# Batch norm and the next layer's products as one stage, with features along the partitions

## The chip, the cores and the metric

The kernel runs on one core of a Trainium2 chip. The metric is the time on the device in microseconds (us), the median of several runs. A core has five engines, each with its own instruction stream: TensorE (PE, with PEld for its weight loads), VectorE (DVE), ScalarE (ACT), GpSimd (POOL) and SyncE (SP). They meet only through semaphores. SyncE and GpSimd issue the DMAs here.

## The reference, cut to what matters

The program runs four graph networks one after the other over 3125 nodes of 256 features and 50000 edges. The change is in the last of them, which has three layers:

```python
for l in range(thetas.shape[0]):
    xi = x[src]
    xj = x[dst]
    e = jax.nn.relu((xj - xi) @ thetas[l].T + xi @ phis[l].T)
    agg = jax.ops.segment_max(e, src, num_segments=N)
    agg = jnp.where(agg < -1e+30, 0.0, agg)
    mu = agg.mean(axis=0)
    var = agg.var(axis=0)
    x = jax.nn.relu((agg - mu) * jax.lax.rsqrt(var + BN_EPS) * gammas[l] + betas[l])
```

Behind it come a residual sum and a layer norm: `x = _layernorm(x + ...)`. The mean and the variance go over the nodes, one of each per feature.

## The kernel before

The nodes lie in 25 tiles of 128 (the last one has 53), each tile with its nodes along the partitions and 256 features behind one another: `X`, `AGG`, `C` and `Y` hold 25 such tiles. Since `xj @ theta` depends on one node alone, a layer forms two products per node. `AGG = x @ theta` goes to a table in memory (`T`), from which the edges gather rows, and `C = x @ (phi - theta)`, the node's own term, stays and is added after the maximum.

Each layer has three stages, and all engines leave a stage together:

- `node_products` (n6, n7, n8 for the three layers). VectorE makes the input rows of a tile, TensorE turns them (two transposes of 128 columns), ScalarE copies them out of PSUM, TensorE makes both products (four matmuls with 256 columns, of which fp32 makes eight records), ScalarE and VectorE copy one product each. For n7 and n8 the rows are made by `stage_normed`, which multiplies by the factor, adds beta and takes the positive part, three VectorE instructions a tile (L1535, L1537, L1539). Every five tiles SyncE stores a piece of the table (L1212).
- `edge_pass` (e5, e6, e7). GpSimd issues 392 indirect gathers of 128 rows each (L1288) into 24 buffers; VectorE runs a maximum over them (L1337); SyncE stores four at a time (L1271). TensorE and ScalarE have nothing to do in these three passes.
- `batch_norm` (bn0, bn1, bn2). GpSimd gathers the maximum of each node (L1447), one DMA a tile. Sums that cross from one partition's chain to the next are mended: VectorE makes a selection matrix (L1497), TensorE multiplies it with the carried rows (L1471), VectorE takes the maximum (L1007). Every five tiles VectorE adds `C` and takes the positive part (L1513, L1514), and TensorE sums over the nodes by a product with ones (L1456). Then the mean is taken off in five wide instructions (L1519), ScalarE squares (L1485), TensorE sums again (L1456), and the factor is made of 256 columns (L1522 to L1526).

Behind bn2 the stage `layer_norm` (ln3) applies the factor and the shift, adds to `X` and takes the row statistics, five tiles at a time (L1417 to L1381), then finds all factors, scales all 25 tiles on ScalarE (L1398), and then stores the output by two DMAs (L1406, L1407).

Of the kernel before, what the change touches and what calls it, by code (L numbers as in the profile page):

```python
# [4 lines left out]
F32 = mybir.dt.float32  # L5
# [8 lines left out]
P = 128  # L14
# [136 lines left out]
def build(nc, a, out):  # L151
    top = ExitStack()
    Stage.used = []
    with top:
# [79 lines left out]
        GAM, BET = sb("GAM", [P, LAYERS, D]), sb("BET", [P, LAYERS, D])  # L234
# [42 lines left out]
        def setup():  # L277
# [17 lines left out]
            with Stage(nc, "set") as st:  # L295
# [43 lines left out]
                def _(eng):  # L339
# [23 lines left out]
                    def spread_row(dst, src, width):  # L363
# [6 lines left out]
                    spread_row(GAM[:, :, :].rearrange("p l d -> p (l d)"),  # L370
                               a["L3_gnn_gammas"].rearrange("(o l) d -> o (l d)", o=1), LAYERS * D)
                    spread_row(BET[:, :, :].rearrange("p l d -> p (l d)"),
                               a["L3_gnn_betas"].rearrange("(o l) d -> o (l d)", o=1), LAYERS * D)
# [973 lines left out]
        def layer_norm(name, prepare, gather=None, out_rows=None):  # L1347

            u = NODE_UNROLL
            with Stage(nc, name) as st:  # L1350
                names = ("chain", "aggregated", "rooted", "scaled", "done", "stored", "apart")
                chain, aggregated, rooted, scaled, done, stored, apart = (st.sem(n) for n in names)
                got = gathered[0:NT // u]
                block = st.block()

                if gather is not None:
                    @block.gpsimd
                    def _(eng):
                        rows, index = gather
                        for t in range(NT):  # L1360
                            got[t % u].arrived(eng, t // u)
                            eng.indirect_dma_start(AGG[:, t, :], None, rows,
                                                   bass.IndirectOffsetOnAxis(ap=index[:, t:t + 1], axis=0)).then_inc(got[t % u].sem, 16)

                @block.vector
                def _(eng):
                    c = Count(eng, chain)
                    with c.loop(NT // u, LINKS[prepare] + 3) as i:
                        if gather is not None:
                            for k in range(u):  # L1370
                                got[k].arrived(eng, i + 1)
                        prepare(c, ds(i * u, u))
                        eng.sem_inc(apart, 1)
                        for j in range(u):
                            last = eng.bn_stats(BS[:, j, :], X[:, ds(i * u + j, 1), :].rearrange("p o d -> p (o d)"))  # L1375
                        c.link(last)
                        eng.sem_inc(apart, 1)
                        for j in range(u):
                            last = eng.bn_aggr(MV5[:, j, :], BS[:, j, :])  # L1379
                        c.link(last)  # L1380
                        c.link(eng.tensor_copy(MV[:, ds(i * u, u), :], MV5[:, :, :]))  # L1381
                    c.link(eng.tensor_scalar(RST[:, :], MV[:, :, 1], EPS, None, ALU.add))
                    eng.sem_inc(aggregated, 1)
                    eng.wait_ge(rooted, 1)
                    c.link(eng.reciprocal(RST[:, :], RST[:, :]))  # L1385
                    c.link(eng.tensor_tensor(NMR[:, :], MV[:, :, 0], RST[:, :], ALU.mult))
                    c.link(eng.tensor_scalar(NMR[:, :], NMR[:, :], -1.0, None, ALU.mult))
                    eng.sem_inc(scaled, 1)

                @block.scalar  # L1390
                def _(eng):
                    eng.wait_ge(aggregated, 1)
                    eng.activation(RST[:, :], RST[:, :], ACT.Sqrt).then_inc(rooted, 1)
                    eng.wait_ge(scaled, 1)
                    with eng.Fori(0, NT // u) as i:  # L1395
                        for j in range(u):
                            t = i * u + j
                            last = eng.activation(tile_of(X, t), tile_of(X, t), ACT.Identity,  # L1398
                                                  bias=NMR[:, ds(t, 1)], scale=RST[:, ds(t, 1)])
                        last.then_inc(done, 1)  # L1400

                if out_rows is not None:
                    @block.sync
                    def _(eng):
                        eng.wait_ge(done, NT // u)
                        eng.dma_start(out_rows[0:(NT - 1) * P, :].rearrange("(t p) d -> p t d", p=P), X[:, 0:NT - 1, :]).then_inc(stored, 16)  # L1406
                        eng.dma_start(out_rows[(NT - 1) * P:N, :], X[0:LAST, NT - 1, :]).then_inc(stored, 16)  # L1407
                        eng.wait_ge(stored, 32)
            if gather is not None:
                for g in got:  # L1410
                    g.close(NODE_UNROLL)


        def last(c, at):

# [10 lines left out]
        def batch_norm(name, layer, gather):  # L1426
# [3 lines left out]
            with Stage(nc, name) as st:  # L1430
# [19 lines left out]
                def column_sums(eng, dst, src, ready, in_front=lambda t: None):  # L1450
                    for t in range(NT):
                        in_front(t + u)
                        if t % u == 0:
                            eng.wait_ge(ready, t // u + 1)
# [481 lines left out]
```

## Time and profile before

| | us |
|---|---|
| median of 3 runs | 5130.29 (5123.8 to 5138.38) |
| the profiled execution, its own time | 5124.81 |
| its span | 5123.1 |
| TensorE busy | 1578.3 (31%) |
| VectorE busy | 3141.9 (61%) |
| ScalarE busy | 1014.3 (20%) |
| GpSimd busy | 3322.2 (65%) |

The busy times are sums over stages that have different limits, so a change in one stage is read from that stage's part of the timeline. A row of the timeline gives the start, the duration of a group, the engine, the line, what is written and read, how many instructions, and in brackets how long the engine was idle before it and what released it. The duration of a pipelined instruction reaches over the start of the next one, so paces are read from starts.

### The profile page before, as it was taken

Reading aid. Unit: us, or ns where it says so; the run is one execution under the profiler, and the core shown is the slowest. Engines: PE = TensorE matmul, PEld = TensorE weight load, DVE = VectorE, ACT = ScalarE, POOL = GpSimd, SP = SyncE. Lnnn points to the kernel's source line nnn. Section 1 sums busy time; section 2 is a strip of 40 time slices with the busy share of each in tenths; the row PEclk is TensorE's granted clock in tenths of the full one; section 3 lists DMA queues with packets and bytes.
Section 4 is the critical chain, followed back from the end, with each engine's and each line's share of the span. In section 5 each row is a group of like instructions: output and inputs, shape, how many; then the busy total and the mean of one; then the engine's idle time right before and its main releaser. Section 6 shows DMA issues by size and latency. Waiting matters only on the chain. (4 is left out here: it accounts for less than half of the span.)

```text
span 5123.1 us, 34834 instructions
## 1 busy us (share of the span) xinstructions
PE 1578.3 (31%) x6898; PEld 1040.1 (20%) x6898; DVE 3141.9 (61%) x9163; ACT 1014.3 (20%) x2570; POOL 3322.2 (65%) x3435
## 2 busy tenths in 40 slices
PE   5220175557555575555400014000070000700002
PEld 5110053335333352222300013000050000500002
DVE  5897566556556579998688887333353333533335
ACT  3333334443444440000311122000010000100001
POOL 3777757774777737777577760777727777177771
PEclk8555575557555595555755557555585555855556
DMA  2766546664666516665366650666516665166661
GB/s 94 229 198 222 189 145 207 208 209 130 202 207 209 193 54 205 205 205 190 91 218 221 222 176 31 201 205 207 192 51 201 207 204 192 49 201 205 205 194 48
DMA packets 318311, 898.86 MB, mean 175 GB/s; under 512 B 73771, under 2 KB 109976, under 8 KB 317976
## 3 DMA queue, kind: packets, MB, share of 16 engines
q0 software_dynamic: 161760, 439.40, 30.8%
q1 hardware_dynamic: 156344, 457.31, 23.9%
q14 instruction: 152, 1.25, 0.1%
q8 instruction: 55, 0.90, 0.1%
HBM read 450.64 MB, written 445.80 MB: 175 GB/s over the span
## 5 line engine op out<-in xcount | busy, mean ns | idle before, releaser
L1288 POOL DMA_INDIRECT WORK<-table,SRCI x1568 | 1512.3, 964 | 638.4 <-issue 512.3
L1288 POOL DMA_INDIRECT WORK<-table,BYSRC x1176 | 1145.6, 974 | 673.0 <-issue 451.0
L1337 DVE SCALAR_TENSOR_TENSOR WORK<-WORK,LOWE 128x256 f32<-128x256 f32 x1564 | 762.9, 488 | 964.4 <-DMA WORK<-table,BYSRC 892.4
L1337 DVE SCALAR_TENSOR_TENSOR WORK<-WORK,NST,e_mv 128x256 f32<-128x256 f32 x1173 | 563.2, 480 | 499.7 <-ACT e_mv L1307 260.2
L1307 ACT ACTIVATE e_mv<-WORK,WE 128x256 f32<-128x256 f32 x1176 | 491.3, 463 | 833.6 <-DMA WORK<-table,SRCI 795.3
L991 PE MATMUL bn_e<-ident,WORK 128*128 128x128 f32 x6 | 2.0, 434 | 1546.2 <-PEq L148 1546.2
L1626 POOL DMA_INDIRECT WORK<-table_attention,SRCI x392 | 373.3, 952 | 119.4 <-issue 119.4
L991 PEld LDWEIGHTS bn_e<-ident,WORK 128*128 128x128 f32 x6 | 0.9, 204 | 1547.3 <-issue 1547.3
L1481 ACT ACTIVATE WORK<-bn_e 128x256 f32<-128x256 f32 x3 | 1.2, 384 | 1551.2 <-PE bn_e L1002 1551.2
L962 PE MATMUL e_hi<-ARENA 128*128 128x392 bf16 x392 | 205.5, 524 | 229.1 <-DVE ARENA L948 229.1
L898 PE MATMUL e_rb<-ARENA 98*128 98x128 bf16 x392 | 114.7, 293 | 444.6 <-ACT ARENA L914 444.6
L900 PE MATMUL e_ra<-ARENA 98*128 98x32 f32 x784 | 249.0, 412 | 0.0
L962 PE MATMUL e_lo<-ARENA 128*128 128x392 bf16 x392 | 208.0, 531 | 0.0
L900 PEld LDWEIGHTS e_ra<-ARENA 98*128 98x128 f32 x784 | 196.2, 310 | 45.8
L898 PEld LDWEIGHTS e_rb<-ARENA 98*128 98x128 bf16 x392 | 95.8, 244 | 462.6 <-ACT ARENA L914 462.6
L1751 DVE SCALAR_TENSOR_TENSOR WORK<-WORK,NST,att_g 128x256 f32<-128x256 f32 x343 | 165.0, 481 | 21.2 <-DVE att_g L1734 10.4
L1158 PE MATMUL n_m<-TURNED,WORK 128*128 128x256 f32 x600 | 163.1, 397 | 0.0
L1786 PE MATMUL comb<-ident,WORK 128*8 128x128 f32 x1 | 0.4, 369 | 527.6 <-PEq L148 527.6
L1162 PE MATMUL n_m<-TURNED,WORK 128*128 128x256 f32 x600 | 155.6, 382 | 0.0
L888 PE MATMUL e_rt<-identb,ARENA 128*98 128x128 bf16 x392 | 132.5, 338 | 12.3 <-DVE ARENA L263 12.3
L1145 PE MATMUL n_x<-WORK 128*128 128x256 f32 x200 | 72.5, 453 | 206.6 <-DVE WORK L1062 198.3
L947 DVE TENSOR_SCALAR ARENA<-iota_b,ARENA 128x128 bf16<-128x128 bf16 x392 | 129.3, 330 | 0.0
(351 smaller groups left out, 4308.5 us busy)
## 6 DMA issues: line engine op xcount, KB each, us to landing
edge_results<-WORK SPq DMA_DIRECT2D x686, 512.0 KB, 3.2
edge_results_attention<-WORK SPq DMA_DIRECT2D x98, 544.0 KB, 3.2
WORK<-table,SRCI POOLq DMA_INDIRECT x1568, 2.9
table<-ARENA SPq DMA_DIRECT2D x35, 640.0 KB, 3.2
WORK<-table,BYSRC POOLq DMA_INDIRECT x1176, 2.9
WORK<-table_attention,SRCI POOLq DMA_INDIRECT x392, 3.3
table_attention<-ARENA SPq DMA_DIRECT2D x5, 660.0 KB
out<-X SPq DMA_DIRECT2D x1, 3072.0 KB
```

The costliest lines, as they stand in the source:

```text
L888: eng.transpose(turned_hot[0:HI, 0, n * P:(n + 1) * P], rank_hi[:, b, n, :], identb[:, :])
L898: eng.matmul(pb[:, cols], rank_t[0:HI, b, 0, cols], rank_t[0:HI, b, 0, cols], start=True, stop=False)
L900: last = eng.matmul(pa[:, n * LO:(n + 1) * LO], rank_tf[0:HI, b, cols], HIST[0:HI, ds((k + first) * RB + n, 1), :].rearrange("p o l -> p ( ...
L947: eng.tensor_scalar(oh_pay[:, b, n, 0, :], iota_b[:, :], place_lo[:, ds(t, 1)], pay_hi[:, ds(t, 1)], ALU.is_equal, ALU.mult)
L962: last = eng.matmul(sums[d][:, :], oh_pay[:, q % 2, n, d, :], oh_place[:, q % 2, n, :], start=False, stop=False)
L1158: last = eng.matmul(mps[:, t % 4, 0:D], XT[:, slot, k * P:(k + 1) * P], w1[:, k, :], start=k == 0, stop=k == 1)
L1162: last = eng.matmul(mps[:, t % 4, D:D + n2], XT[:, slot, k * P:(k + 1) * P], w2[:, k, :], start=k == 0, stop=k == 1)
L1288: eng.indirect_dma_start(G[:, q * GT + k, 0:D], None, T, bass.IndirectOffsetOnAxis(ap=index[:, t:t + 1], axis=0)).then_inc(got[q].sem, 16)
L1307: last = eng.activation(bank[:, k * D:(k + 1) * D], G[:, first + k, 0:D], ACT.Copy, scale=WE[:, ds(g * GT + (2 * h + k), 1)])
L1337: eng.scalar_tensor_tensor(O[:, q % OB, k, :], behind, mask[:, ds(g * GT + k, 1)], here, op0, op1).then_inc(linked, 1)
L1626: eng.indirect_dma_start(G[:, q * GT + k, :], None, T2, bass.IndirectOffsetOnAxis(ap=SRCI[:, t:t + 1], axis=0)).then_inc(got[q].sem, 16)
L1751: eng.scalar_tensor_tensor(OA[:, i, t, 0:D], OA[:, i, t - 1, 0:D] if t else scaled_row, NST[:, ds(b * BT + t, 1)], here, ALU.mult, ALU.add ...
```

## The change

In the third network's place in the order nothing moves up to n6 and e5. Then:

- bn0 and n7 become one stage, and so do bn1 and n8. bn2 and ln3 become one stage too.
- In the first part of the new stage TensorE turns each tile as soon as it is mended: a product of a block of `AGG` with the identity, and on top of it the same for `C`, so that the addition of `C` is made in PSUM. ScalarE takes the positive part on the way out, into `YT`, which has features along the partitions. VectorE takes the sums by `bn_stats` over 512 nodes at a time.
- Then factor and shift are two numbers per partition. ScalarE applies both and the positive part in ten instructions, and `YT` is already turned as the next product wants it.
- Only the product for the table is made in the stage. The own term's product and its copy to `C` are made beside the next edge pass, on TensorE and ScalarE (`own_term_beside`).
- In the last layer TensorE turns the tiles back, VectorE adds them to `X`, and the layer norm goes by fives with a store behind each five.
- gammas and betas are loaded as single numbers down the partitions instead of as rows spread over all partitions.

```diff
-                    spread_row(GAM[:, :, :].rearrange("p l d -> p (l d)"),
-                               a["L3_gnn_gammas"].rearrange("(o l) d -> o (l d)", o=1), LAYERS * D)
...
+                        eng.dma_start(GAMT[:, :], a["L3_gnn_gammas"].rearrange("l (k p) -> p (l k)", p=P)).then_inc(rest_in, 16)
+                        eng.dma_start(BETT[:, :], a["L3_gnn_betas"].rearrange("l (k p) -> p (l k)", p=P)).then_inc(rest_in, 16)
...
+                    def turn(t):
+                        n = P if t < NT - 1 else LAST
+                        eng.wait_ge(mended, t + 1)
+                        if t >= 2:
+                            eng.wait_ge(evicted, t - 1)
+                        for k in range(2):
+                            at = slice(k * P, (k + 1) * P)
+                            eng.matmul(tps[:, t % 2, at], AGG[0:n, t, at], ident[0:n, :], start=True, stop=False)
+                            last = eng.matmul(tps[:, t % 2, at], C[0:n, t, at], ident[0:n, :], start=False, stop=True)
+                        last.then_inc(turned, 1)
...
                     for t in range(NT):
...
+                        nodes = slice(t * P, (t + 1) * P)
                         if t % u == 0:
...
+                            eng.wait_ge(normed, (t // u + 1) * 2)
+                        if t >= 4:
+                            eng.wait_ge(moved, t - 3)
+                        for k in range(2):
+                            if w1 is not None:
+                                last = eng.matmul(ps[:, t % 4, 0:D], YT[:, k, nodes], w1[:, k, :], start=k == 0, stop=k == 1)
+                            else:
+                                last = eng.transpose(ps[:, t % 4, k * P:(k + 1) * P], YT[:, k, nodes], ident[:, :])
...
+                    eng.wait_ge(rooted, 3)
+                    for c in range(NT // u):
+                        nodes = slice(c * u * P, (c + 1) * u * P)
+                        for k in range(2):
+                            eng.activation(YT[:, k, nodes], YT[:, k, nodes], ACT.Relu, bias=BF[:, k, 1:2], scale=BF[:, k, 0:1]).then_inc(normed, 1)
+                    if w1 is None:
+                        for c in range(NT // u):
+                            at = slice(c * u, (c + 1) * u)
+                            eng.wait_ge(spread, c + 1)
+                            eng.activation(RST[:, at], RST[:, at], ACT.Sqrt).then_inc(rooted_rows, 1)
+                            eng.wait_ge(scaled_rows, c + 1)
+                            for t in range(c * u, (c + 1) * u):
+                                eng.activation(X[:, t, :], X[:, t, :], ACT.Identity, bias=NMR[:, t:t + 1], scale=RST[:, t:t + 1]).then_inc(done, 1)
...
+                    def sums(j):
+
+                        eng.wait_ge(evicted, min(4 * j + 4, NT))
+                        for k in range(2):
+                            c.inc(eng.bn_stats(BNS[:, k, j, :], YT[:, k, 4 * j * P:min((4 * j + 4) * P, N)]))
...
+                    def rows_of(k):
+                        for t in range(k * u, (k + 1) * u):
+                            eng.wait_ge(made, t + 1)
+                            eng.tensor_tensor(X[:, t, :], ps[:, t % 4, 0:D], X[:, t, :], ALU.add).then_inc(moved, 1)
+                        eng.wait_ge(moved, (k + 1) * u)
+                        for j in range(u):
+                            last = c.inc(eng.bn_stats(BS[:, j, :], X[:, k * u + j, :]))
+                        c.wait()
+                        for j in range(u):
+                            c.inc(eng.bn_aggr(MV[:, k * u + j, :], BS[:, j, :]))
...
                     for k in range(NT // u):
...
+                        rows_of(k)
+                        if k:
+                            factors_of(k - 1)
+                    factors_of(NT // u - 1)
...
+                def on_tensor(eng):
+                    def multiply(g, q, turn):
+                        if g < NT:
+                            if g >= 2:
+                                eng.wait_ge(moved, g - 1)
+                            for k in range(2):
+                                last = eng.matmul(own[:, g % 2, 0:D], YT[:, k, g * P:(g + 1) * P], DF3[:, layer, k, :], start=k == 0, stop=k == 1)
+                            last.then_inc(made, 1)
```

On TensorE, at the start of bn0, the order before alternates a selection's product (L1471, of 256 columns) with a column sum (L1456):

```order
L991 MATMUL bn_e<-ident,WORK 128x128 x2
L1002 MATMUL bn_e<-ident,WORK 128x128 x2
L1471 MATMUL bn_x<-WORK 128x256 x6
L1456 MATMUL bn_ps<-ARENA,ones 128x256
L1471 MATMUL bn_x<-WORK 128x256
L1456 MATMUL bn_ps<-ARENA,ones 128x256
L1471 MATMUL bn_x<-WORK 128x256
```

On TensorE at the same place the order after has, for each selection's product (L1384), four products of 128 columns with the identity (`bn_t` is the turned tile, L1393 from `AGG`, L1394 from `C`):

```order
L990 MATMUL bn_ps<-ident,WORK 128x128 x2
L1001 MATMUL bn_ps<-ident,WORK 128x128 x2
L1384 MATMUL bn_ps<-WORK 128x256 x2
L1393 MATMUL bn_t<-ident,ARENA 128x128
L1394 MATMUL bn_t<-ident,ARENA 128x128
L1393 MATMUL bn_t<-ident,ARENA 128x128
L1394 MATMUL bn_t<-ident,ARENA 128x128
L1384 MATMUL bn_ps<-WORK 128x256
L1393 MATMUL bn_t<-ident,ARENA 128x128
```

So the column sums have gone and four short products stand in each tile's place. On ScalarE the whole of the new stage and the piece beside the edge pass stand in a few rows, where n7 alone had two copies a tile before (L1418 copies the carried rows, L1421 takes the tile out of PSUM, L1424 is the root, L1429 applies factor and shift, L1551 is the own term's copy):

```order
L1418 ACTIVATE WORK<-bn_ps 128x256
L1421 ACTIVATE ARENA<-bn_t 128x2x128 x25
L1424 ACTIVATE BF<-BF 128x2
L1429 ACTIVATE ARENA<-ARENA,BF 128x640 x10
L148 UNCONDITIONAL_BRANCH
L1298 UNCONDITIONAL_BRANCH
L1551 ACTIVATE ARENA<-e_own 128x256 x25
```

The copies of the table's product are no longer among them: VectorE makes them now (L1483). On TensorE, at the start of n7, the order before was this, for each tile two transposes and both products (L1158 the table's, L1162 the own term's):

```order
L1151 MATMUL n_t<-ident,WORK 128x128 x4
L1158 MATMUL n_m<-TURNED,WORK 128x256 x2
L1162 MATMUL n_m<-TURNED,WORK 128x256 x2
L1151 MATMUL n_t<-ident,WORK 128x128 x2
L1158 MATMUL n_m<-TURNED,WORK 128x256 x2
L1162 MATMUL n_m<-TURNED,WORK 128x256 x2
```

and after, the 25 products for the table (two matmuls each) stand behind the last turned tile, and the own term's 50 matmuls have moved into the next edge pass:

```order
L1393 MATMUL bn_t<-ident,ARENA 128x128
L1394 MATMUL bn_t<-ident,ARENA 128x128
L1410 MATMUL bn_ps<-TURNED,ARENA 128x256 x50
L148 UNCONDITIONAL_BRANCH
L1290 UNCONDITIONAL_BRANCH
L1543 MATMUL e_own<-TURNED,ARENA 128x256 x50
```

The transposes of n7 are gone, and the own term's products stand in a stage in which TensorE had no row before.

## Rows read from the trace of the kernel before

**Rows 1.** Windows: start:end, length, PE, PEld, DVE, ACT, POOL busy (count), clock, DMA, GB/s
```profile
3706.80:3753.00 46.20, 29.37 (x104) 21.72 (x104) 29.29 (x63) 0.38 (x1) 26.33 (x25) 0.81 0.24 71
3753.00:3774.00 21.00, 14.13 (x50) 11.39 (x50) 9.88 (x9) 6.77 (x6) 0.00 (x0) 0.79 0.00 1
3774.00:3836.60 62.60, 53.09 (x250) 41.52 (x250) 36.97 (x100) 17.86 (x50) 0.02 (x1) 0.94 0.15 53
4989.30:5055.00 65.70, 42.48 (x154) 32.36 (x154) 39.01 (x71) 7.15 (x7) 25.60 (x25) 0.83 0.17 51
5055.00:5096.00 41.00, 0.00 (x0) 0.00 (x0) 34.68 (x73) 0.22 (x1) 0.00 (x0) 0.51 0.00 0
5109.00:5123.00 14.00, 0.00 (x0) 0.00 (x0) 0.00 (x0) 0.14 (x1) 0.00 (x0) 0.50 0.69 229
```

**Rows 2.** Timeline of GpSimd and VectorE as the first batch norm begins
```profile
3707.56 0.94 POOL L1447 DMA_INDIRECT ARENA<-edge_results,end_src  x1 [9.53 <-SPq L148]
...
3712.55 0.94 POOL L1447 DMA_INDIRECT ARENA<-edge_results,end_src  x1 [0.30 <-issue]
...
3715.48 0.48 DVE L1007 SCALAR_TENSOR_TENSOR ARENA<-bn_x,ALONE,ARENA 128x256 f32<-128x256 f32 x1 [6.22 <-DMA ARENA<-edge_results,end_src]
...
3716.07 0.48 DVE L1007 SCALAR_TENSOR_TENSOR ARENA<-bn_x,ALONE,ARENA 128x256 f32<-128x256 f32 x1
```

**Rows 3.** Timeline of TensorE: products of 256 columns, then selections beside loads
```profile
3056.17 0.69 PE L1794 MATMUL comb_x<-WORK 128*128 128x264 f32 x2
...
3056.69 0.29 PE L1795 MATMUL comb_x<-WORK 128*128 128x8 f32 x2
...
3056.83 0.69 PE L1794 MATMUL comb_x<-WORK 128*128 128x264 f32 x2
...
3829.24 1.03 PE L1158 MATMUL n_m<-TURNED,WORK 128*128 128x256 f32 x4
...
3830.10 1.03 PE L1162 MATMUL n_m<-TURNED,WORK 128*128 128x256 f32 x4
```

**Rows 4.** Windows of the batch norm's first part, columns as in rows 1
```profile
3721.00:3725.00 4.00, 4.00 (x11) 3.29 (x12) 1.60 (x5) 0.00 (x0) 3.03 (x4) 0.58 0.33 98
3725.00:3740.00 15.00, 10.40 (x48) 8.51 (x47) 12.46 (x28) 0.00 (x0) 11.90 (x11) 1.00 0.33 97
```

**Rows 5.** Timeline of TensorE: the 25 column sums of squares after a pause
```profile
3756.07 14.13 PE L1456 MATMUL bn_ps<-ARENA,ones 128*128 128x256 f32 x50 [3.34 <-ACT ARENA L1485]
```

**Rows 6.** Timeline of ScalarE and VectorE: squares, a row's statistics, the factors, the scaling
```profile
3754.74 6.88 ACT L1485 ACTIVATE ARENA<-ARENA 128x1280 f32<-128x1280 f32 x5 [45.28 <-DVE ARENA L1519]
...
5060.51 1.73 DVE L1375 BATCH_NORM_STATS2 BS<-X 128x6 f32 x5
5062.38 0.45 DVE L1379 BATCH_NORM_AGGREGATE MV<-BS 128x2 f32<-128x6 f32 x5
...
5095.07 0.18 DVE L1382 TENSOR_SCALAR ROWSUMS<-ROWSUMS 128x25 f32<-128x25 f32 x1 [0.21 <-DVE ROWSUMS L1381]
...
5096.76 12.39 ACT L1398 ACTIVATE X<-X,ROWSUMS  x25 [1.19 <-DVEq L1388]
```

**Rows 7.** Timeline: the last copy of a product, and the next pass's first gather
```profile
3831.69 0.42 DVE L1900 COPY ARENA<-n_m 128x256 f32<-128x256 f32 x1 [1.30 <-ACT ARENA L1545]
3836.58 0.94 POOL L1288 DMA_INDIRECT WORK<-table,BYSRC  x1 [95.39 <-PEq L148]
```

**Rows 8.** Timeline of GpSimd: first and last gather of passes one and six
```profile
120.74 1.12 POOL L1288 DMA_INDIRECT WORK<-table,SRCI  x1 [36.80 <-issue]
...
613.99 0.94 POOL L1288 DMA_INDIRECT WORK<-table,SRCI  x1 [0.30 <-issue]
...
4336.01 1.12 POOL L1288 DMA_INDIRECT WORK<-table,BYSRC  x1 [0.30 <-issue]
```

**Rows 9.** Timeline of SyncE's queue in the setup: a bias, and the tables
```profile
21.23 7.14 SPq L352 DMA_DIRECT2D WORK<-in_L_gnn_fc_b  x1
...
94.58 21.84 SPq L383 DMA_DIRECT2D table<-ARENA  x5
```

More of the change, by code:

```diff
@@ L1353, in layer_norm @@
                 got = gathered[0:NT // u]
[L1354 to L1411, printed above, removed]
@@ L1448, in _ @@
                                                bass.IndirectOffsetOnAxis(ap=index[:, t:t + 1], axis=0)).then_inc(got[t % u].sem, 16)
[L1450 to L1454, printed above, removed]
-                        n = P if t < NT - 1 else LAST
-                        last = eng.matmul(dst, ones[0:n, :], src[0:n, t, :], start=t == 0, stop=t == NT - 1)
-                    last.then_inc(summed, 1)
@@ L1523, in _ @@
[L1523 to L1540 removed]
+                    for t in range(NT):
+                        got[t % u].arrived(eng, t // u + 1)
+                        eng.wait_ge(crossed, t + 1)
+                        mend_max(eng, t, ps[:, 2 + t % 2, 0:D], 1).then_inc(mended, 1)
+                        if t + u < NT:
+                            select(t + u)
+                        if t % 4 == 1 and t > 4:
+                            sums(t // 4 - 1)
@@ new lines, in _ @@
+                    c.link(eng.tensor_tensor(BF[:, :, 0], BF[:, :, 0], GAMT[:, 2 * layer:2 * layer + 2], ALU.mult))
+                    c.link(eng.tensor_tensor(BF[:, :, 1], BMV[:, :, 0], BF[:, :, 0], ALU.mult))
+                    c.link(eng.tensor_tensor(BF[:, :, 1], BETT[:, 2 * layer:2 * layer + 2], BF[:, :, 1], ALU.subtract))
+                    eng.sem_inc(rooted, 1)
+                    if w1 is not None:
+                        for t in range(NT):
+                            eng.wait_ge(made, t + 1)
+                            eng.tensor_copy(AGG[:, t, :], ps[:, t % 4, 0:D]).then_inc(moved, 1)
+                        return
@@ new lines, in batch_norm, with own_term_beside, beside, on_scalar @@
+            for g in got:
+                g.close(u)
+        def own_term_beside(layer):
+            def beside(st, name):
+                made, moved = st.sem("own_made"), st.sem("own_moved")
+                own = st.stack.enter_context(nc.psum_tensor(f"{name}_own", [P, 2, 512], F32))
+                def on_tensor(eng):
[3 more added lines that the diff above has]
+                                eng.wait_ge(moved, g - 1)
+                            for k in range(2):
+                                last = eng.matmul(own[:, g % 2, 0:D], YT[:, k, g * P:(g + 1) * P], DF3[:, layer, k, :], start=k == 0, stop=k == 1)
+                            last.then_inc(made, 1)
+                    return [], [(multiply, 0)]
+                def on_scalar(eng):
+                    def move(g, q, turn):
+                        if g < NT:
+                            eng.wait_ge(made, g + 1)
+                            eng.activation(C[:, g, 0:D], own[:, g % 2, 0:D], ACT.Copy).then_inc(moved, 1)
+                    return [], [(move, 0)]
+                return dict(tensor=on_tensor, scalar=on_scalar)
+            return beside
```

159 lines of the change are left out of this document (75 added, 84 removed).

## The prediction

> **What bounds the kernel now.** I read the windows first [rows 1]. Between two edge passes lie three stretches: 46.2 us in which gathers, mending and the first column sums run together, 21.0 us for the deviations, squares and factors, and 62.6 us for n7 with the restart of the gathers. Together they are 129.8 us, from 3706.8 to 3836.6, and the same comes again behind e6. GpSimd, which paces the edge passes, is idle in the second and third stretch. In the second, VectorE works 9.88 us, ScalarE 6.77 and TensorE 14.13, largely one behind the other. In the third TensorE is busy for 53.09 of 62.6 us, so it is the bound there, with four products of 256 columns and two transposes a tile. Behind the last pass there are 133.8 us (4989.3 to 5123.1). VectorE alone fills 41 us of it, ScalarE's scaling takes 12.39 us [rows 6], and the store 14 us, and these three follow each other.
>
> **The change, middle layers.** I count from the stage's start at 3706.8.
>
> The first gather is issued at 0.8, lands 2.93 us after its issue (3712.55 to 3715.48) and gathers follow every 1.25 us [rows 2]. So tile 0 is there at 3.7, mended at 4.2, and the last gather lands at 0.8 + 24 x 1.25 + 2.9 = 33.7. VectorE needs 0.59 us for a mending and a selection (start to start of two, 3715.48 to 3716.07) [rows 2]. To it come two `bn_stats` of 512 columns for four tiles; five of 256 took 1.73 us [rows 6], 0.35 each, so one of 512 lies between 0.35 and 0.70, and I take 0.61: 0.3 a tile. VectorE then has 0.9 us a tile and isn't the bound.
>
> TensorE per tile: a product of 256 columns costs 0.43 us at the full clock (four of these records in 0.86 us, 3829.24 to 3830.10, two records a product) [rows 3]. Four products of 128 columns are eight records, which the trace before doesn't have. Columns alone make half of 0.215, so 0.108 each. The load could cost more: between 3056.17 and 3056.83 two records of 264 columns and two of 8 columns take 0.66 us [rows 3]; the long ones are 0.44, which leaves 0.11 for a load with hardly a column behind it. Load and columns are of one size, then. Hidden behind each other they make 0.11 a record, one after the other 0.22. In the long products the load is hidden, so I take 0.11: 8 x 0.11 + 0.43 = 1.31 us a tile, against 2.15 at the other end. TensorE, not the gathers, then paces this part.
>
> At half clock a tile takes 2.6 us. Before, the clock stood at 0.58 from 3721 to 3725, with TensorE busy all four microseconds, and at 1.00 from then on, with TensorE busy 10.40 of 15 us [rows 4]. Now TensorE is busier than that and starts at 4.3. I give the half clock 5 us and two tiles, then 23 x 1.31 = 30.1: the last tile is turned at 39.4. ScalarE's copy adds 0.5, the last 53 nodes' statistics 0.35, two aggregations 0.35: 40.6. The factor is now two numbers per partition instead of 256. The same chain stands in ln3: from the addition of eps at 5095.07 over the root to the scaling at 5096.76 are 1.69 us [rows 6]; with one more small step 1.9. That makes 42.5. The stages before needed 67.2 to that point.
>
> The first two scalings of 640 columns come next. Five of 1280 took 6.88 us, 1.38 each, and one of 256 took 12.39/25 = 0.50 [rows 6]; in between 640 is 0.5 to 1.38, and by the slope between them 0.82. So 1.7 with the wait: 44.2. The other eight run ahead of TensorE. Its 25 tiles cost 0.86 us each, 21.5. The clock has dropped by then: the 25 sums of squares, 10.8 us at full clock, took 14.13 us after a pause of 3.34 us [rows 5], 3.3 more; the bounds are 0 and 3.5, I take 2.6. So 68.3. VectorE's copies of 0.42 [rows 7] fit beside it, only the last counts, 0.7 with its waits: 69.0. From the end of the last copy (3832.11) to the next gather (3836.58) were 4.5 us [rows 7], with the store of the last fifth in it; it stays. 73.5 instead of 129.8: **56.3 us less, twice, 112.6**.
>
> The own term's 50 products and 25 copies move to a pass in which TensorE and ScalarE were idle. At half clock they are 43 us of its 510. What covers them is GpSimd's pace. Pass one had TensorE, ScalarE and VectorE at work beside it, and its gathers took 493.3 us from first to last (120.74 to 613.99); pass six, with nothing on TensorE and ScalarE, took 499.4 (3836.58 to 4336.01) [rows 7, 8]. I count nothing.
>
> **The last layer.** To 42.5 the same. The first pair of scalings and the first transposes: 44.9. Then VectorE paces, per five tiles five additions from PSUM at 0.4 (the copies there take 0.42 singly), statistics 1.73, aggregation 0.45 [rows 6], and 0.6 for small steps and waits: 4.8, and for three of them 0.45 for the factors of the five before: 25.3, so 70.2. Then come in line: the factors of the fourth five 0.45, their scaling 2.5, root and factors of the last five 0.8, their scaling 2.5: 76.5. The last store was 14 us for all rows [rows 1]; a fifth of it is bounded by the 4.5 us of the table's restart below and 14 above; since the 53 rows come last in a DMA of their own as before, I take 6.0. 82.5 instead of 133.8: **51.3 us less**.
>
> **The setup.** Two loads of 768 single numbers each take the place of two broadcasts. The bias that is loaded in this manner held the queue 7.14 us [rows 9]. Two of them put off what stands behind by some 14 us, from 46 to 60, and the queue's next duty is at 94.58 [rows 9]. Hidden; without that cover 14 us.
>
> **Sum.** 112.6 + 51.3 = 163.9. The profiled execution took 5124.8, 5.5 below the median of 5130.3. 5124.8 - 163.9 = 4960.9, and in the median's terms **4966 us**.
>
> **Rivals.**
> Weight loads that don't hide. Eight short records with a new load each never stood in a row before; if load and columns follow each other, a tile takes 2.15 us instead of 1.31, 23 x 0.84 = 19.3 us in each of three stages: 4966 + 58 = 5024. For it: load and column time are equal, so nothing is left over to absorb a gap. Against it: the 8-column records show loads at 0.11 right behind each other. 12 in 100. The Trainium skill, page "TensorE: Matmul & The Clock Gate", section "Back-to-back issue gap", holds that in a stream of load and matmul pairs a 128-column matmul comes every 81 ns where it would take 56 alone; by that ratio of 1.45 the stages would lose about 9 us each, an estimate of some 4992. No row before shows such a stream, and the rows stand nearer to the hidden load.
>
> A clock that stays at half. Then a tile takes 2.6 us, 65 us for 25 instead of 35, and the products 43 instead of 24: 3 x 30 + 2 x 19 = 128, 5094. The clock before rose in a thinner stretch [rows 4], so 3 in 100.
>
> Slower than before: the own term beside e6 and e7 delays the gathers, by reading and writing the same memory. That decides from (164 + 15)/784 = 0.23 us a gather on, 1.27 to 1.50, through both passes, although it lasts only for their first tenth. At 0.25 it would be 5162. Pass one speaks against it [rows 8]. 2 in 100.
>
> The element loads end the setup later, up to 14 us: 4980. 4 in 100.
>
> **How the numbers follow.** The forecast as worked out has 79 in 100; its own range is 4952 (the clock rises at once and doesn't fall, 5 us a stage) to 4990 (8 us more for the last store, 5 a stage for waits between mending and turning). To hold 8 in 10 I reach to part of the first rival: 4950 to 5004. About 0.3%, 15 us, is what a measurement can tell from no change. Faster 0.97, same 0.01, slower 0.02.
>
> **What would show it.** The four short products should start some 0.22 us apart at full clock, and a tile come every 1.3 us; at 2.1 the first rival holds. The factor should be ready near 42.5 us after the stage's start, the first product 2 us later, the next gather at 73 to 74. The gathers of e6 and e7 should keep 1.27 us. The last stage should show VectorE without pauses, and the store's end near 82 us. I would be wrong if VectorE's statistics, waiting on ScalarE's copies, hold up the next mending and so TensorE, or if the last stage's chain between VectorE and ScalarE has waits that I put at tenths.

## The result and the profile after

The changed kernel takes 4959.26 us (median of 4 runs, 4953.19 to 4963.35) against 5127.05 us of the kernel before (5119.34 to 5138.38): ratio 0.967, interval 0.9648 to 0.9693. The forecast was 4966. The profiled execution took 4953.19 us, 171.6 less than the one before; the sum of terms said 163.9. The page of the profile, with span and busy time:

```profile
span 4951.5 us, 34938 instructions
PE 1527.9 (31%) x7148; PEld 1041.6 (21%) x7148; DVE 3038.7 (61%) x9035; ACT 1032.0 (21%) x2614; POOL 3314.2 (67%) x3435
```

The windows of the new stage behind e5, columns as in [rows 1], which they answer:

```profile
3704.30:3710.00 5.70, 4.28 (x13) 2.81 (x14) 3.10 (x11) 0.38 (x1) 3.77 (x4) 0.50 0.25 70
3710.00:3714.00 4.00, 4.00 (x25) 3.77 (x25) 1.28 (x4) 0.77 (x2) 2.98 (x4) 0.76 0.37 102
3714.00:3746.00 32.00, 29.30 (x220) 27.37 (x218) 22.04 (x59) 9.04 (x24) 16.88 (x18) 1.00 0.27 79
3746.00:3748.00 2.00, 0.06 (x1) 0.07 (x1) 0.06 (x1) 1.85 (x3) 0.00 (x0) 0.52 0.00 0
3748.00:3752.00 4.00, 4.00 (x10) 3.19 (x11) 0.67 (x2) 4.00 (x6) 0.00 (x0) 0.50 0.00 0
3752.00:3755.00 3.00, 3.00 (x13) 2.57 (x12) 1.04 (x4) 2.38 (x3) 0.00 (x0) 0.85 0.00 0
3755.00:3773.80 18.80, 17.22 (x80) 14.82 (x78) 8.92 (x21) 0.00 (x0) 0.00 (x0) 1.00 0.41 142
```

The last column but two is the granted clock. TensorE is busy for 29.30 of 32 us in the first part and nearly without a break in the products; between them it pauses (0.06 of 2 us), and behind the pause it runs at half clock until some 3752.9 (a mean of 0.85 over the three microseconds from 3752). Its timeline within one tile of the first part, in which the reader is to see the starts: a selection's product at 3715.34, four short pairs 0.22 us apart, the next tile's product at 3716.67. It answers to [rows 3].

```profile
3715.34 0.60 PE L1384 MATMUL bn_ps<-WORK 128*128 128x256 f32 x2
3715.78 0.38 PE L1393 MATMUL bn_t<-ident,ARENA 128*128 128x128 f32 x2
3716.00 0.39 PE L1394 MATMUL bn_t<-ident,ARENA 128*128 128x128 f32 x2
3716.22 0.39 PE L1393 MATMUL bn_t<-ident,ARENA 128*128 128x128 f32 x2
3716.45 0.39 PE L1394 MATMUL bn_t<-ident,ARENA 128*128 128x128 f32 x2
3716.64 1.28 DVE L1452 BATCH_NORM_STATS2 BNS<-ARENA 128x6 f32<-128x512 f32 x2
3716.67 0.60 PE L1384 MATMUL bn_ps<-WORK 128*128 128x256 f32 x2
```

The chain from the last turned tile to the first products, and from the last copy to the gather of e6, which answers to [rows 6, 7]:

```profile
3743.03 0.38 PE L1394 MATMUL bn_t<-ident,ARENA 53*128 53x128 f32 x2
3744.23 0.55 DVE L1470 BATCH_NORM_AGGREGATE BMV<-BNS 128x2 f32<-128x42 f32 x2
3746.15 6.60 ACT L1429 ACTIVATE ARENA<-ARENA,BF 128x640 f32<-128x640 f32 x8 [0.88 <-DVEq L1479]
3747.94 4.63 PE L1410 MATMUL bn_ps<-TURNED,ARENA 128*128 128x256 f32 x10 [4.53 <-ACT ARENA L1429]
3750.05 0.42 DVE L1483 COPY ARENA<-bn_ps 128x256 f32<-128x256 f32 x1 [3.99 <-PE bn_ps L1410]
3751.76 0.42 DVE L1483 COPY ARENA<-bn_ps 128x256 f32<-128x256 f32 x1 [1.28 <-PE bn_ps L1410]
3772.26 0.42 DVE L1483 COPY ARENA<-bn_ps 128x256 f32<-128x256 f32 x1 [0.44 <-PE bn_ps L1410]
3777.17 0.94 POOL L1287 DMA_INDIRECT WORK<-table,BYSRC  x1 [41.12 <-issue]
```

And the end of the last stage, with the scaling of the fourth and the last five tiles (L1437), the root of the last five (L1434) and the last store:

```profile
4939.48 2.56 ACT L1437 ACTIVATE X<-X,ROWSUMS 128x256 f32<-128x256 f32 x5 [2.22 <-DVEq L1506]
4941.95 0.19 ACT L1434 ACTIVATE ROWSUMS<-ROWSUMS 128x5 f32<-128x5 f32 x1
4942.65 2.56 ACT L1437 ACTIVATE X<-X,ROWSUMS 128x256 f32<-128x256 f32 x5 [0.51 <-DVEq L1506]
4945.65 0.36 SPq L1526 DMA_DIRECT2D out<-X  x1
```

Counted from the stage's first product (3704.39, then 4287.67 and 4870.49) the next gather comes at 72.8 and 73.0, and the end at 81.0. Before it was 129.8, 132.7 and 133.8. That is 57.0 + 59.7 + 52.8 = 169.5 of the 171.6 us. The rest is that e5 started 2.6 us sooner, in a part of which the change touches only two loads of the setup, less some tenths in the passes.

Of the 57.0 us of the first stage 25.4 stand before the factors (the scaling starts at 41.8, where 67.2 us were needed) and 31.6 behind them (31.0 instead of 62.6).

### The profile page after: what moved, and what is told of

Read it like the earlier page. It is cut to its first block and busy times, and to the rows that moved or that the text cites. A ratio compares the mean times of both kernels' runs of the same rounds, so it can differ in the third digit from the quotient of the medians.

```text
span 4951.5 us, 34938 instructions
## 1 busy us (share of the span) xinstructions
PE 1527.9 (31%) x7148; PEld 1041.6 (21%) x7148; DVE 3038.7 (61%) x9035; ACT 1032.0 (21%) x2614; POOL 3314.2 (67%) x3435
## 3 DMA queue, kind: packets, MB, share of 16 engines
q0 software_dynamic: 161760, 439.40, 31.9%
## 5 line engine op out<-in xcount | busy, mean ns | idle before, releaser
L1418 ACT ACTIVATE WORK<-bn_ps 128x256 f32<-128x256 f32 x3 | 1.2, 384 | 1495.2 <-PE bn_ps L1001 1495.2
L961 PE MATMUL e_hi<-ARENA 128*128 128x392 bf16 x392 | 185.1, 472 | 262.4 <-DVE ARENA L947 262.4
L961 PE MATMUL e_lo<-ARENA 128*128 128x392 bf16 x392 | 186.7, 476 | 0.0
L945 DVE TENSOR_SCALAR ARENA<-iota_h,ARENA 128x392 bf16<-128x392 f16 x392 | 128.6, 328 | 0.2 <-DVEq L938 0.2
L961 PEld LDWEIGHTS e_hi<-ARENA 128*128 128x128 bf16 x392 | 49.8, 127 | 365.7 <-DVE ARENA L947 322.9
```

The lines of the kernel that those rows point to most:

```text
L945: eng.tensor_scalar(oh_place[:, b, n, :], iota_h[:, :], place_hi[:, ds(t, 1)], None, ALU.is_equal)
L961: last = eng.matmul(sums[d][:, :], oh_pay[:, q % 2, n, d, :], oh_place[:, q % 2, n, :], start=False, stop=False)
```

## The experiments

Four of the twelve ran on a chip where the kernel before takes 5137.9 us, about what it takes above (below, a quick chip). The other eight fell on three further chips, below called the slower chips: four on one where it takes 5970 us, three on one where it takes 6018, and the last on one where it takes 6017 and 6025. Totals are compared with the kernel before on the same chip, and stages by their traces. A stage that no edit touched differs from execution to execution: in the run with the own term in all 98 steps the three stages took 72.1, 71.9 and 80.1 us, where the kernel after's took 72.8, 73.0 and 81.0.

**The own term back in the stage.** Its products stand beside the table's again and nothing stands beside e6 and e7; a second copy a tile goes to VectorE.

```diff
+                            for k in range(2):
+                                last = eng.matmul(ps[:, t % 4, D:2 * D], YT[:, k, nodes], DF3[:, layer + 1, k, :], start=k == 0, stop=k == 1)
...
+                            eng.tensor_copy(C[:, t, 0:D], ps[:, t % 4, D:2 * D]).then_inc(moved, 1)
...
-                edge_pass(f"e{5 + l}", BYSRC, (ALU.add, ALU.max), LOWE, False, own_term_beside(l) if l else nothing_beside)
+                edge_pass(f"e{5 + l}", BYSRC, (ALU.add, ALU.max), LOWE, False)
```

> The changed kernel with one part undone: the own term's product goes back into the stage, behind the table's product of the same tile (TensorE two more matmuls of 256 columns a tile, VectorE one more copy), and nothing stands beside passes six and seven. If TensorE paces the products (theory): 25 x 0.86 = 21.5 us more in each of two stages, next gather some 94 us after the stage's start instead of 72.8, in all 4959 + 43 = 5002. If the move itself was worth nothing (rival: something else, such as ScalarE's scalings or the copies, paces the products), 4959 to 4965.

5003.31 us, ratio 0.9744 (0.9725 to 0.9762). The copies of a tile come 1.73 us apart instead of 0.86, and the gather of e6 starts 93.4 us after the stage's start instead of 72.8; behind e6 it is 95.2. The window and the gather:

```profile
3750.00:3800.00 50.00, 45.43 (x200) 39.34 (x200) 19.55 (x54) 8.28 (x11) 0.00 (x0) 0.93 0.15 53
3803.43 0.95 POOL L1287 DMA_INDIRECT WORK<-table,BYSRC  x1 [61.66 <-PEq L148]
```

The move beside the pass is worth 20.6 and 22.2 us a stage, the whole TensorE time of 50 products (25 x 0.86 = 21.5). It is a quarter of the gain; the rest is in the one-stage form, whose terms (no deviations, no second sums, factors of two numbers, rows that are turned already) no experiment takes apart: they rest on the sum and the trace.

**A third short product for each half of a tile in the turning.** It writes a bank that nobody reads.

```diff
...
+                            eng.matmul(spare[:, at], AGG[0:n, t, at], ident[0:n, :], start=True, stop=True)
```

> The changed kernel with two further products of 128 columns a tile in the first part (AGG's two blocks with the identity once more, into a PSUM bank that nobody reads). If TensorE paces the first part with hidden weight loads (theory): four more records of 0.11, 0.44 us for each of the 25 tiles, 11 us a stage, 4959 + 33 = 4992, and the tile's pace 1.77 instead of 1.33. If the gathers or VectorE pace it and TensorE has slack (rival), under 2 us a stage, 4959 to 4965.

4999.19 us, ratio 0.9729 (0.9711 to 0.9747). The tiles come 1.77 us apart instead of 1.33:

```profile
3746.49 0.60 PE L1385 MATMUL bn_ps<-WORK 128*128 128x256 f32 x2
3748.26 0.60 PE L1385 MATMUL bn_ps<-WORK 128*128 128x256 f32 x2
```

The stages are 9.4, 9.0 and 11.1 us longer. The added product is made for either half of the columns, 0.22 us each, so 25 x 0.44 = 11. Up to the aggregation of the column statistics, ahead of which the edit stands, it is 10.1, 9.9 and 11.0 us; the middle stages' products behind it took 0.7 and 0.9 us less than in the kernel after, though nothing was changed there. TensorE sets the pace of the first part: it had no slack that would have swallowed the pair.

**The own term in all 98 steps of e6 and e7** (the same values are written again), four times the load of the change.

```diff
-                        if g < NT:
+                        n = g % NT
+                        if g < NG:
...
```

> The changed kernel with the own term's product and copy made in all 98 steps of passes six and seven, not in the first 25 (the same values are written again). If TensorE and ScalarE are covered by the gathers (theory): no change, 4959, each pass 510 us from its first gather to the next stage. If they delay the gathers through the memory (the rival of a loss): four times the disturbance; at 0.02 us a gather, which the two profiles could not tell, 16 us more, 4975; at 0.23 some 180 more.

4966.25 us, ratio 0.9671 (0.9653 to 0.9689), not told apart from the kernel after. The pass e6 with this load, then that of the next experiment with the normal load, each from its first gather to the next stage's first weight load:

```profile
3779.96 0.94 POOL L1287 DMA_INDIRECT WORK<-table,BYSRC  x1 [40.27 <-issue]
4291.82 0.29 PEld L990 LDWEIGHTS bn_ps<-ident,WORK 128*128 128x128 f32 x2 [426.54 <-issue]
```

```profile
3781.67 0.95 POOL L1287 DMA_INDIRECT WORK<-table,BYSRC  x1 [37.89 <-issue]
4293.95 0.29 PEld L990 LDWEIGHTS bn_ps<-ident,WORK 128*128 128x128 f32 x2 [489.00 <-issue]
```

511.9 and 512.3 us. The rival that the own term slows the gathers is refuted on this chip, with four times its dose. On the slower chips told of below the passes took 538.4 and 538.7 us in the kernel after and 537.1 twice in the kernel before, on different chips and once each, so there a delay of 1.3 us a pass is not excluded.

**Twenty spare products while the factors are made**, between the last turned tile and the first product.

```diff
...
+                    for _ in range(20):
+                        eng.matmul(spare[:, 0:P], ident[:, :], ident[:, :], start=True, stop=True)
```

> The changed kernel with 20 products of the identity with itself (128 columns) between the last turned tile and the first product, into a bank that nobody reads, so that TensorE is not idle for the 4.5 us. If the pause is what lets the clock fall (theory): the products run at the full clock from the first, 24 us become 21.5 in two stages, some 2.3 us less each, 4954, which the profile can show and the median hardly. If the clock falls all the same (rival), no change, and the first three tiles still come 1.7 us apart.

4960.66 us, ratio 0.9657 (0.9641 to 0.9673). The totals can't tell 0.9657 from the 0.9671 of the run before, the trace can:

```profile
3750.00:3752.00 2.00, 2.00 (x18) 1.88 (x18) 1.83 (x7) 0.39 (x2) 0.00 (x0) 1.00 0.04 8
3752.00:3755.00 3.00, 3.00 (x28) 2.94 (x28) 0.65 (x4) 2.12 (x4) 0.00 (x0) 1.00 0.00 0
3755.00:3777.00 22.00, 21.71 (x100) 18.77 (x100) 10.45 (x25) 6.30 (x8) 0.00 (x0) 1.00 0.34 120
3756.03 0.42 DVE L1486 COPY ARENA<-bn_ps 128x256 f32<-128x256 f32 x1 [3.05 <-PE bn_ps L1413]
3756.89 0.42 DVE L1486 COPY ARENA<-bn_ps 128x256 f32<-128x256 f32 x1 [0.44 <-PE bn_ps L1413]
```

The clock stays at 1.00, and the copies are 0.86 us apart from the first on, where they were 1.71 and then 1.51 (the rows at 3750.05 and 3751.76 above). The stages are 69.7, 70.4 and 79.0 us against 72.8, 73.0 and 81.0, 7.8 us together, but 2.2 of these stand ahead of the aggregation, where nothing was changed. From the aggregation to the gather it is 30.5 us in both middle stages instead of 32.9 and 33.1 (32.7 in both in the run before, on the same chip). So the pause cost 2.2 to 2.6 us of half clock in each of them. In the last stage, from the aggregation to the end, it is 40.0 instead of 40.6.

**The turning without the own term**, which is left out of the output too.

```diff
-                            eng.matmul(tps[:, t % 2, at], AGG[0:n, t, at], ident[0:n, :], start=True, stop=False)
-                            last = eng.matmul(tps[:, t % 2, at], C[0:n, t, at], ident[0:n, :], start=False, stop=True)
+                            last = eng.matmul(tps[:, t % 2, at], AGG[0:n, t, at], ident[0:n, :], start=True, stop=True)
```

> Only the batch-norm stage's turning is changed: the products that add the nodes' own term are left out (its output leaves the own term out), so a tile costs TensorE some 0.44 us less, 0.88 us instead of 1.32. Theory (TensorE paces part one, and the gathers, 1.25 us apart, stand close behind it): the pace goes to 1.25 us and no further, the last tile is turned some 3 us earlier in each of the three stages, 4950 us. Rival (the turning's pace falls to TensorE's own 0.88, the gathers run ahead): 11 us a stage, 4926. Rival (another wait sets the pace, and TensorE only fills it): 4959, no change.

5839.18 us, ratio 0.9791 (0.9739 to 0.9842), on a slower chip, so the total answers none of the three. There the rows of part one come late and then all at once, which gives TensorE's pace without the gathers: four tiles in 4.44 us.

```profile
4505.36 0.47 DVE L1006 SCALAR_TENSOR_TENSOR ARENA<-bn_ps,ALONE,ARENA 128x256 f32<-128x256 f32 x1
4509.80 0.47 DVE L1006 SCALAR_TENSOR_TENSOR ARENA<-bn_ps,ALONE,ARENA 128x256 f32<-128x256 f32 x1
```

The full kernel after in the same condition (from a run on another slower chip, told below) needs 5.34 for four:

```profile
4526.52 0.47 DVE L1006 SCALAR_TENSOR_TENSOR ARENA<-bn_ps,ALONE,ARENA 128x256 f32<-128x256 f32 x1
4531.86 0.47 DVE L1006 SCALAR_TENSOR_TENSOR ARENA<-bn_ps,ALONE,ARENA 128x256 f32<-128x256 f32 x1
```

1.33 a tile with every row at hand is the pace of the kernel after's own run, where the gathers were in time: they don't set it. With one pair less it is 1.11 and not 0.88, as VectorE's statistics, 1.28 us every fourth tile, now hold up a mending: the second of these rows starts 1.79 us behind the mending before it, and TensorE's next pair waits for it.

**Small first chunks, a small last store.** ScalarE scales 1, 1, 2, then 4 tiles; the table's last five tiles are stored as four and one.

```diff
+        scale_at = [0, 1, 2, 4, 8, 12, 16, 20, NT]
+        store_at = [0, 5, 10, 15, 20, 24, NT]
...
```

> ScalarE's first scalings in part two are made small (1, 1, 2, then 4 tiles) so that the first product starts some 1.1 us sooner, and the last five tiles of the table are stored as four and one. Theory (first product is on the chain, and the last piece's 640 KB at some 350 GB/s too): 1.1 us in each of three stages and 1.4 in each of two, 4953 us. Rival (TensorE's clock comes back to full only some time after the first product, so the sooner start runs at half speed as long as before; the landing is latency and not bytes): 3.3 us at most, 4956 to 4959.

5858.58 us on the same slower chip, ratio 0.9822 (0.977 to 0.9874). From the aggregation to the next gather it is 31.0 and 30.2 us. In the experiments before and behind this one, on the same chip and with this part of the kernel after unchanged, it is 33.6 and 31.9, and 33.6 and 32.5. The first product starts 2.9 us behind the aggregation instead of 3.7, and the gather stands 4.0 us behind the start of the last copy instead of 4.9, in both stages. So both terms are there, 0.85 and 0.9 us where 1.1 and 1.4 were expected, though the unchanged stages scatter by 1.7 us. In the last stage the small scalings cost time: from the aggregation to the end it is 41.3 us instead of 40.6.

**The last stage's end.** The roots are taken sooner, VectorE scales the last two tiles beside ScalarE, and the last 53 rows are stored as 48 and 5.

```diff
-                            at = slice(c * u, (c + 1) * u)
+                            if c < NT // u - 2:
+                                root_rows(c + 1)
...
+                    for t in range(NT - 2, NT):
+                        eng.tensor_scalar(X[:, t, :], X[:, t, :], RST[:, t:t + 1], NMR[:, t:t + 1], ALU.mult, ALU.add).then_inc(done_v, 1)
...
```

> Only the last stage's end is changed: ScalarE makes the last five's root before the fourth five's scalings are queued in front of it, the fourth five's factors are made before the last five's sums, VectorE scales the last two tiles beside ScalarE, and the last 53 rows are stored as 48 and 5. Theory (scaling chain 4 us, and the 53 rows move through few DMA engines, some 2 us): end of the stage 75.5 us after its start instead of 81.0, 4954 us. Rival (the last store's 5.9 us is latency whatever its rows): 3.5 us, 4956.

5850.64 us on the same chip, ratio 0.9815 (0.9763 to 0.9866). The trace's end of this kernel (span 5845.4):

```profile
5834.14 5.02 ACT L1443 ACTIVATE X<-X,ROWSUMS 128x256 f32<-128x256 f32 x10 [0.33 <-DVEq L1512]
5839.78 1.58 ACT L1443 ACTIVATE X<-X,ROWSUMS 128x256 f32<-128x256 f32 x3 [0.51 <-DVEq L1512]
5839.84 0.73 DVE L1522 TENSOR_SCALAR X<-X,ROWSUMS 128x256 f32<-128x256 f32 x2 [0.15 <-DVE ROWSUMS L1511]
5841.80 0.50 SPq L1538 DMA_DIRECT2D out<-X  x1
```

From the aggregation of the column statistics to the end it is 35.0 us instead of 40.6: 5.7 us less, where 5.5 was expected. The last scaling ends 3.4 us sooner, and from the issue of the last 53 rows' first store (of 48 rows) to the end it is 3.6 us instead of 5.8. The rival of pure latency falls.

**All three.**

> The kernel after, with 14 spare products that keep TensorE busy while the factors are made, the small chunks, and the changed end of the last stage. If the three gains add: 8 for the clock, 6 for the chunks, 5.4 for the end, 4940 us (0.963 of the kernel before). If clock and chunks are the same gain counted twice: 4944.

5836.76 us on the same chip, ratio 0.9781 (0.9738 to 0.9824). The middle stages need 28.9 us from aggregation to gather, both; the last 35.3, no better than with its end alone. There the tiles are only turned back, which is quick, and small scalings made TensorE wait for ScalarE.

**All three, with 2, 3 and then five tiles a scaling in the last stage**, beside the kernel after and the turning without the own term once more. All three fell on a slower chip again, the second of them.

> All three edits again, with the small chunks only where products follow (the last stage scales 2, 3, and then five tiles at once). On a chip whose passes are as long as in the kernel after's own run, every term has its reading: the stage shortened by 3 us for the clock and 2 for the chunks, twice; the last stage by 5.6 for its end and 0.5 to 1 for its first chunk: 16 us less than the kernel after on the same chip, 4943 us, ratio 0.9640 where that of the kernel after is 0.967. Rival (clock and chunks count the same time twice): 4947.

> The kernel after, unchanged, beside the others on one chip: ratio 0.967 to the kernel before if that chip's transfers are as quick as in its first run; 0.979 if they are as slow as in the second set of experiments.

> The turning without the nodes' own term (left out of the output too) once more, on a chip where the gathers land in time. Where all rows had landed long before, its pace was 1.11 us a tile, against 1.33 of the full one. Theory: now the gathers' 1.25 us bind and the last tile is turned 3 us sooner a stage, 9 to 10 us in all against the kernel after on the same chip. Rival (1.11 is reached here too): 15 us.

5877.47 us (5864.19 to 5883.38), ratio 0.9763 (0.9741 to 0.9786), against 5900.81 (5885.12 to 5904.14), ratio 0.98 (0.9777 to 0.9823), of the kernel after on the same chip; 5868.9, ratio 0.9744 (0.9718 to 0.9771), for the one with a pair less, whose stages are 7.0, 9.7 and 10.2 us shorter than the kernel after's. From aggregation to gather it is 28.9 us twice, against 31.9 and 33.6, and 34.2 to the end, against 40.7: 14.2 us by the trace, where 16 was expected. The clock and the chunks add: with the spare products alone it was 30.5, and of the further 1.6 us half is the sooner first product and half the smaller last store. The 14.2 us lie between the theory's 16 and the rival's 12, as the chunks give 1.6 where 2 was put and the clock some 2.3 where 3 was. This is the fastest full computation on that chip, by 23 us. The question put to the last one (do the gathers bind at 1.25 us?) stays open, as it ran on no chip where the rows are taken up in time.

**The kernel before, for its trace on a slower chip.** On the second of these chips the kernel after keeps 117 us of the gain (5900.81 against 6017.82, ratio 0.98), where it was 168 by the medians and 171.6 between the two profiled executions.

> The kernel before, unchanged, for its trace: on the chip of the last two sets the kernel after kept only 117 of the 171 us. There its stage took 110 us from the first product to the next pass's gather instead of 73, because the landing of the third and the fourth gather was noticed 20 us late each. Theory (the stage of before runs its rows through VectorE in 43 us and hides part of that lateness, so it grows less): 130 becomes 145 to 150, and the missing 54 us are in the stages, 18 each. Rival (before's stage grows by 37 too, and the missing time is in setup or the passes): 167.

6024.92 us, a single execution on the third of the slower chips. In the kernel after's run on the second of them two rows of the stage are taken up some twenty microseconds late each:

```profile
4494.80 0.48 DVE L1006 SCALAR_TENSOR_TENSOR ARENA<-bn_ps,ALONE,ARENA 128x256 f32<-128x256 f32 x1 [19.46 <-DMA edge_results<-WORK]
4515.10 0.48 DVE L1006 SCALAR_TENSOR_TENSOR ARENA<-bn_ps,ALONE,ARENA 128x256 f32<-128x256 f32 x1 [19.62 <-DMA edge_results<-WORK]
```

The profile puts both waits down to a DMA, a store of the pass before. They are not waits for the gathers. GpSimd waits for the same semaphore, and for the same value, ahead of the gather five rows further on as VectorE does ahead of the mending. So when the ninth gather was issued, at 4480.52, the fourth had landed, and the product that the fourth row also needs starts at 4480.97; VectorE took the row up at 4515.10. ScalarE came late too: TensorE had finished the first turned tile by 4478.7, and its copy starts at 4489.13.

```profile
4480.52 0.95 POOL L1370 DMA_INDIRECT ARENA<-edge_results,end_src  x1 [0.30 <-issue]
4480.97 1.06 PE L1384 MATMUL bn_ps<-WORK 128*128 128x256 f32 x2
4489.13 0.38 ACT L1421 ACTIVATE ARENA<-bn_t 128x256 f32<-128x256 f32 x1 [16.71 <-remote]
```

The kernel before resumes as late, at 44.6 us after its first gather of the stage as there, but has mended eight rows by then, not three:

```profile
4498.65 0.48 DVE L1007 SCALAR_TENSOR_TENSOR ARENA<-bn_x,ALONE,ARENA 128x256 f32<-128x256 f32 x1 [9.71 <-issue]
4513.38 0.48 DVE L1007 SCALAR_TENSOR_TENSOR ARENA<-bn_x,ALONE,ARENA 128x256 f32<-128x256 f32 x1 [3.55 <-remote]
```

From the stage's first gather to the next pass's, before takes 157.7, 159.9 and (to the end) 161.1 us, after 109.0, 111.1 and 118.9. The three stages of before have grown by 28.7, 28.0 and 28.1 us against the executions on a quick chip, those of after by 36.9, 38.8 and 38.7. The first of before, 158.4 us from its first product, lies between the theory's 145 to 150 and the rival's 167. So 139.7 us are saved in the stages instead of 169.5: of what is missing, 29.8 us are here, half of what this theory claimed. The remainder of its 54 isn't in the stages: between the two profiled executions (6023.2 and 5888.1 us) 135.1 us are saved. These two ran on different chips, once each, and single runs of the kernel before on the first of the slower chips lie up to 77 us apart. What holds VectorE and ScalarE up the trace doesn't tell, and the cause stays open.

## Why the prediction was right

**Terms of the middle stages.** The tile costs 1.33 us where 1.31 was forecast: eight short records 0.11 apart, so load and columns hide behind each other, and the rival of unhidden loads, 2.15, falls. The Trainium skill's ratio of 81 to 56 for such pairs ("TensorE: Matmul & The Clock Gate", "Back-to-back issue gap"), by the estimate 4992, isn't seen in these rows: a record costs the 0.11 us of its columns alone. The extra pair confirms that this pace is on the path. The last tile is turned at 39.0 for 39.4, the scaling starts at 41.8 for 42.5, the first product stands at 43.5 for 44.2, the last copy ends at 68.3 for 69.0, the gather is at 72.8 for 73.5. The lead of 0.7 us has two sources. The half clock ended some 7.5 us after the stage's start (a mean of 0.76 already from 3710 to 3714), where the sum had it until 9.3. And from the aggregations to the scaling it was 1.9 us (3744.23 to 3746.15), where 0.35 and 1.9 were put one behind the other. The scaling of 640 columns took 0.82 us, as interpolated. The statistics of 512 columns took 0.64 for 0.61.

**The half clock of the products.** 2.6 us was forecast, and the spare products gave back 2.2 to 2.6.

**The own term.** Nothing beside the pass: right, e6 and e7 took 510.5 and 509.8 us against 509.4 and 510.7 before, paced by gathers as in [rows 8], and the load of 98 steps changed nothing.

**The same gain twice** was 2.7 us short: the second stage of before was 132.7 us and not the first one's 129.8, which the prediction took for both.

**The last stage.** 81.0 for 82.5. The first rows came at 44.8 for 44.9. Five tiles with the factors of the five before cost VectorE 4.88 us and without them 4.35, where 4.8 was put without them: the small steps and waits, 0.32 us for 0.6, and the five additions, 1.78 for 2.0, were the mis-sized parts. So VectorE was through at 68.5 for 70.2. The chain of scalings behind it took 6.2 for 6.3, and from its end to the last store's landing were 6.3 for 6.0.

**The setup.** Right in the sum and mis-sized in the part: the queue was free at 55.2 instead of 48.8, 6 us later and not 14, and the tables followed at 95.50 for 94.58 [rows 9]. The loads of single numbers didn't cost it 7.14 each:

```profile
45.79 0.43 SPq L371 DMA_DIRECT2D GAMT<-in_L_gnn_gammas  x1
46.27 2.03 SPq L372 DMA_DIRECT2D BETT<-in_L_gnn_betas  x1
```

**What was luck.** The sum of terms was 5.6 us short of the 169.5 that the stages gave: 0.7 and 3.4 in the middle stages, 1.5 in the last. A further 2.6 us, e5's sooner start, came from no term, and the distance of the median, 4959.26 against 4966, is within what executions of one kernel differ by.

The range was set for one chip. On a slower chip the change is worth 2.0 and not 3.3 in a hundred, and nothing in the prediction said that the gain leans on VectorE and ScalarE taking up their rows in time.

## What to carry to other kernels

Where a pass is paced by one engine's gathers, work of idle engines that only the stage behind the pass needs belongs beside it: here that alone gave 21 us a stage, and four times as much was free on a quick chip. When a stage is cut to little more than its chain, look at what the chain idles: a pause of 4.5 us on TensorE cost some 2.4 us more behind it, and filling it with spare products gave them back. A shorter stage hides less of a lateness that strikes all versions alike, so measure a gain on the slowest chip as well as on the quickest. And when a row is late, look who else waits for the same semaphore before you blame the transfer.

## What was unexpected of the hardware

TensorE's granted clock was already back at half (0.52 from 3746 to 3748) in a pause of 4.5 us between two stretches of full work, and it stood at 0.50 through four microseconds in which TensorE was busy without a break, then at 0.85 and 1.00.

On the two slower chips where it ran, every full kernel of the new form took up the third and the fourth row of a stage some 20 us late each, while GpSimd, which waits for the same semaphores, issued all 25 gathers in 31 us. With one pair less in the turning and the same gathers the late rows are the third, the fourth and the fifth, at some 14, 31 and 44 us. In ten microseconds ahead of the fourth row no byte moved:

```profile
4506.00:4516.00 10.00, 0.36 (x1) 0.36 (x2) 0.90 (x3) 0.77 (x2) 0.00 (x0) 0.50 0.00 0
```

The DMA of 53 rows that ends the kernel after moved its bytes at 4 to 25 GB/s, where 128-row tiles go at some 350. The mean busy share of the 16 DMA engines was 0.06 from 4947.75 to 4950.5, what one of them alone would give, and 0.97 from 4946.1 to 4947.7. In forty slices from 4940 to the end:

```profile
GB/s 32 0 0 0 0 0 0 0 0 0 199 356 349 342 345 342 317 29 0 0 0 185 349 349 349 349 246 4 4 4 25 21 25 25 25 25 21 7 0 0
```
